# Cross-attention and a two-expert FFN on one core: the weights' loads and splits moved into the first batch

## The reference

```python
# attention: q = layernorm(x), k = v = ctx; 8 heads of 16 rows, softmax over 256 keys
qk = einsum('bhdq,bhdl->bhql', qh, kh) / sqrt(16)
x = x + gamma * einsum('bhql,bhdl->bhdq', softmax(qk), vh)
# FFN on xn = layernorm(x): two experts, each 256 -> 512 -> 256, chosen for each row by argmax
h0 = gelu(xn @ W0a.T + b0a);  out0 = h0 @ W0b.T + b0b
h1 = relu(xn @ W1a.T + b1a);  out1 = h1 @ W1b.T + b1b
x = x + where(argmax(xn @ Wg.T) == 0, out0, out1)
```

## Time and profile before

| what | value |
|---|---|
| time, median of 3 runs | 248.42 us (248.38 to 250.54) |
| time of the profiled execution | 248.95 us |
| its span | 247.1 us |
| PE busy | 219.7 us (89%) |
| DVE busy | 178.1 us (72%) |
| ACT busy | 144.6 us (59%) |
| POOL busy | 96.3 us (39%) |
| moved by DMA | 25.86 MB, 105 GB/s on average |

### The profile page before, as it was taken

The page is one execution under the profiler, slowest core; times in us unless marked ns, Lnnn a source line. Parts: engine busy times, 40 slices in busy tenths (PEclk is TensorE's granted clock), DMA queues, the critical chain, the costliest instruction groups (busy, mean ns, idle before and its releaser), DMA issues.

```text
span 247.1 us, 5173 instructions
## 1 busy us (share of the span) xinstructions
PE 219.7 (89%) x2001; PEld 171.3 (69%) x2001; DVE 178.1 (72%) x368; ACT 144.6 (59%) x217; POOL 96.3 (39%) x128
## 2 busy tenths in 40 slices
PE   0477988777898999999999999999999989979995
PEld 0344544444577888788878887888788877959995
DVE  7667476999875988698869886987597715445573
ACT  2012454856667758775877587758774786644140
POOL 8440231333984822482248224823361054032000
PEclk9999999886799999999999999999999999999999
DMA  4227777723330525161516250514111000000101
GB/s 170 100 71 246 247 298 224 273 90 129 88 131 36 183 66 175 10 233 64 176 25 216 65 175 21 178 49 150 20 49 53 16 24 3 21 21 3 41 5 42
DMA packets 18954, 25.86 MB, mean 105 GB/s; under 512 B 1946, under 2 KB 12530, under 8 KB 18674
## 3 DMA queue, kind: packets, MB, share of 16 engines
q1 hardware_dynamic: 17782, 22.63, 27.8%
q10 hardware_dynamic: 1148, 2.90, 3.3%
HBM read 11.28 MB, written 2.10 MB: 54 GB/s over the span
## 4 chain that ended last, share of the span: by engine, by line
PE 72%; DVE 12%; ACT 9%; issue 5%; POOL 0%; DVEq 0%; ACTq 0%; POOLq 0%
PE ff L822 18%; PE ff L852 11%; PE od L765 8%; PE st L753 8%; PE ff L863 6%; PE smax L741 5%; DVE nmax L396 4%; ACT P L600 4%; PE st L728 3%; PE od L773 3%; ACT hid L637 2%; PE od L780 2%; PE smax L714 2%; PE tr L795 1%; DVE qkst L184 1%
## 5 line engine op out<-in xcount | busy, mean ns | idle before, releaser
L600 ACT ACTIVATE P<-st 128x1024 f32<-128x1024 f32 x64 | 65.6, 1025 | 54.1 <-PE st L753 45.6
L396 DVE TENSOR_REDUCE nmax<-smax 128x4 f32<-128x1024 f32 x54 | 66.1, 1224 | 28.8 <-PE smax L741 28.2
L262 POOL TENSOR_TENSOR mv<-mv,power 128x1 f32<-128x1 f32 x31 | 18.3, 591 | 69.2 <-DVE mv L361 69.2
L280 POOL TENSOR_TENSOR hidL<-hid,hidH 128x1024 fp32r<-128x1024 f32 x13 | 31.0, 2387 | 20.6 <-DVE hidH L456 16.2
L822 PE MATMUL ff<-xnTh,w1h 128*128 128x256 f32 x128 | 37.5, 293 | 1.0 <-DVE y L494 1.0
L753 PE MATMUL st<-qkst 64*128 64x256 f32 x240 | 31.1, 338 | 6.6 <-ACT P L600 6.5
L637 ACT ACTIVATE hid<-ff,b1t 128x256 f32<-128x256 f32 x64 | 26.7, 470 | 17.4 <-PE ff L822 17.3
L822 PE MATMUL ff<-xnTh,w1l 128*128 128x256 f32 x128 | 36.0, 281 | 0.0
L822 PE MATMUL ff<-xnTl,w1h 128*128 128x256 f32 x128 | 35.9, 281 | 0.0
L765 PE MATMUL od<-P,vt 128*32 128x256 f32 x512 | 35.7, 426 | 0.1
L852 PE MATMUL ff<-w2h,hidH 128*128 128x256 f32 x124 | 34.2, 309 | 0.0
(11 more groups left out here) (100 smaller groups left out, 344.8 us busy)
## 6 DMA issues: line engine op xcount, KB each, us to landing
qkst<-parts SPq DMA_DIRECT2D x45, 256.0 KB
xv<-in_xv SPq DMA_DIRECT2D x16, 256.0 KB, 2.8
qk<-in_qk SPq DMA_DIRECT2D x15, 256.0 KB, 3.6
out<-y SPq DMA_DIRECT2D x16, 128.0 KB, 2.5
w1t<-in_w ACTq DMA_DIRECT2D x1, 1024.0 KB, 5.4
w2t<-in_w ACTq DMA_DIRECT2D x1, 1024.0 KB, 4.7
qk<-in_first SPq DMA_DIRECT2D x1, 256.0 KB, 3.8
qk<-in_first ACTq DMA_DIRECT2D x1, 256.0 KB, 3.9
```

The costliest lines, as they stand in the source:

```text
L262: pool.tensor_tensor(mv[:, b % 2, 11:12], mv[:, b % 2, 10:11], power[:, 0:1], ALU.pow).then_inc(s_rstd, 1)
L280: pool.tensor_tensor(hidL[:, units, :], hid[:, units, :], hidH[:, units, :], ALU.subtract).then_inc(s_hidL, 1)
L396: dve.tensor_reduce(nmax[:, c % 2, :, :, j].rearrange("p a e -> p e a"), (ff if c in WIDE and j % 2 else smax)[:, :, :, :], AX.X, ALU.max, ...
L600: act.activation(P[:, b % 2, j, :, :, :].rearrange("p e a l -> p (e a l)"), st[:, :, :, :].rearrange("p e a l -> p (e a l)"), ACT.Exp, sca ...
```

## The change

- `EARLY` gives batch 2 the slot -4 instead of -7. Its statistics, its q_norm, its high and low part and its stack copies come three slots later.
- ACT fills place 1 of `qkst` by two ACTIVATEs that read a broadcast constant; DVE fills place 2 alone, and makes the small memset of `onesb` in the head.
- ACT issues the load of w1 ahead of its loop, when the q and k of batch 2 have landed, and makes both halves of its high part there. The load of w2 is issued when the first stack (batch 1) has landed. ACT splits w2 in slots -1 and 0. The four small loads go from slot 0 to slot -2.
- POOL makes the low part of w1 ahead of its loop, before the `rstd` of batch 2, and that of w2 in slots 0 and 1.
- DVE's seven steps for gate and bias go from slots 6 to 12 to slots 0 to 6.

The diff, cut to its core:

```diff
-EARLY = {2: -7, 3: -2}
+EARLY = {2: -4, 3: -2}
@@ gpsimd, ahead of the loop, after the low part of batch 1's q
+            for half in range(LC):
+                pool.wait_ge(s_w1h, half + 1)
+                pool.tensor_tensor(w1l[:, half, :, :], w1t[:, half, :, :], w1h[:, half, :, :], ALU.subtract).then_inc(s_w1l, 1)
             rstd(2, mv1, 2, s_var1, s_rstd1)
@@ gpsimd, in the loop
                 if n == -1:
                     pad_values(0)
+                if 0 <= n < 2:
+                    pool.wait_ge(s_w2h, n + 1)
+                    half = slice(n * HM, (n + 1) * HM)
+                    pool.tensor_tensor(w2l[:, half, :], w2t[:, half, :], w2h[:, half, :], ALU.subtract).then_inc(s_w2l, 1)
...
-                if b == 3 and j >= 2:
-                    pool.wait_ge(s_w2h, j - 1)
-                    half = slice((j - 2) * HM, (j - 1) * HM)
-                    pool.tensor_tensor(w2l[:, half, :], w2t[:, half, :], w2h[:, half, :], ALU.subtract).then_inc(s_w2l, 1)
-                if b == 3 and j < LC:
-                    pool.wait_ge(s_w1h, j + 1)
-                    pool.tensor_tensor(w1l[:, j, :, :], w1t[:, j, :, :], w1h[:, j, :, :], ALU.subtract).then_inc(s_w1l, 1)
@@ vector
-            fill(dve, 1)
+            dve.memset(onesb[:, :], 1.0).then_inc(s_ones, 1)
             fill(dve, 2)
...
-                if 6 <= n < 13:
-                    gate_and_bias(n - 6)
+                if 0 <= n < 7:
+                    gate_and_bias(n)
@@ scalar, ahead of the loop
             act.dma_start(qk0[:, :, 1, :], first[1].rearrange("p (h l) -> p h l", h=2)).then_inc(s_c0, 16)
+            act.wait_ge(s_const, 1)
+            for side in range(2):
+
+                act.activation(qkst[:, 1, :, side, :], power[:, 0:1].unsqueeze(2).to_broadcast([128, PAIRS, L]), ACT.Copy,
+                               scale=-2.0 * side).then_inc(s_fill[1], 1)
             act.wait_ge(s_qk[0], 16)
...
             act.dma_start(qk0[DH:128:32, :, 1, :], ones0[:, :, :]).then_inc(s_one0, 16)
+
+            act.wait_ge(s_qk[1], 16)
+            act.dma_start(w1t[:, :, :, :].rearrange("p a e f -> p (a e f)"), w1).then_inc(s_w1, 16)
             act.wait_ge(s_qn, 1)
             act.activation(parts[:, 1, 1, :], qk[:, 0, 0, :], ACT.Copy).then_inc(s_hi, 1)
+            act.wait_ge(s_w1, 16)
+            for half in range(LC):
+                act.activation(w1h[:, half, :, :], w1t[:, half, :, :], ACT.Copy).then_inc(s_w1h, 1)
+            act.wait_ge(s_stk[0], stacked(1))
+            act.dma_start(w2t[:, :, :].rearrange("p u l -> p (u l)"), w2).then_inc(s_w2, 16)
@@ scalar, in the loop, after exp and copy_max0
-                if n == 0:
+                if -1 <= n < 1:
+                    act.wait_ge(s_w2, 16)
+                    half = slice((n + 1) * HM, (n + 2) * HM)
+                    act.activation(w2h[:, half, :], w2t[:, half, :], ACT.Copy).then_inc(s_w2h, 1)
+                for p in prepared(n - 2 if n > 0 else n - 1) if n else ():
+                    high(p)
+                if n == -2:
                     act.dma_start(wgb[:, :, :].rearrange("p a c -> p (a c)"), wg.partition_broadcast(128)).then_inc(s_small, 16)
...
```

More of the change, by code:

```diff
@@ L513, in gate_and_bias @@
                 if step == 5:
-                    dve.memset(onesb[:, :], 1.0).then_inc(s_ones, 1)
-                    dve.memset(bias_rows[:, :], 0.0).then_inc(s_ones, 1)
+                    dve.memset(bias_rows[:, :], 0.0).then_inc(s_bias, 1)
                 if step == 6:
-                    dve.wait_ge(s_bias, 4)
-                    dve.wait_ge(s_ones, 2)
+                    dve.wait_ge(s_bias, 5)
                     for n in range(3):
                         dve.tensor_copy(bias_rows[32 * n:32 * n + 1, :], bias_p[32 * n:32 * n + 1, n, :]).then_inc(s_bias, 1)
-            fill(dve, 1)
+            dve.memset(onesb[:, :], 1.0).then_inc(s_ones, 1)
             fill(dve, 2)
@@ L667, in _ @@
                     act.dma_start(b1t[:, :], b1).then_inc(s_small, 16)
[L668 to L680, removed]
                 if k == 0 and 2 <= c <= B:
@@ L830, in begin @@
                     pe.wait_ge(s_w2, 16)
-                    pe.wait_ge(s_bias, 7)
-                    pe.wait_ge(s_ones, 2)
+                    pe.wait_ge(s_bias, 8)
+                    pe.wait_ge(s_ones, 1)
                 pe.wait_ge(s_hid, UNITS * (b // 2) + (UNITS if t else UNITS - 2))
```

## The result

| | kernel before | changed kernel |
|---|---|---|
| median of 20 runs | 249.0 us (247.99 to 251.71) | 247.64 us (246.42 to 249.47) |
| ratio | 1 | 0.9937 (95% interval 0.9912 to 0.9963) |
| span of the profiled execution | 247.1 us | 246.3 us |

The change makes the kernel 0.6% faster, 1.6 us, where 0.4 us slower was forecast. The ratio lies near that of the means (249.3 and 247.8 us); the medians lie 1.4 us apart. The size is within 1%, as forecast most likely, but the interval excludes no change, and the sign is the other one.

A forecast was written before the change was run, and what follows sets the result against it. DVE was taken to bound the first third and PE the rest, so the first gemm's start decides. Terms -0.35 + 0.15 + 1.3 + 0.55 - 1.25 = +0.4 us gave a 248.8 us median, range 246.4 to 250.9.

The forecast's parts named there:

- part 1, the head: Fills, loads and statistics up to 17 us: ACT's fills let POOL's first pow start about 0.35 us earlier.
- the paragraph on the sum: Added the terms to +0.4 us at values(2); after it, x_norm's and q_norm's lost waits lie beside PE.
- Part 2: Early weight loads and splits: w1 lands near 11.9 us, POOL's split ends by 17.7; only w2's load costs, 0.15 us.
- Rival B: Slower: w1's load and the stack copies collide, w1 lands up to 3 us late, +2.25, 251.05 us; chance 0.10.
- Part 3: Port between DVE and POOL: POOL's w2 split blocks q_norm(4), perhaps the gate step; 0.65 to 1.1 us, 0.85 taken.
- Parts 3 and 4: Port blocking plus DVE's bias steps between the maxima: PE's transpose of batch 2 and values(0) come 1.3 us late.
- Part 5: DVE-bound stretch, n = 7 to 12: the steps that left it give back 1.25 us of chain.
- step 6: DVE's three copies, 0.90 us, between q_norm(5) and maximum (3,2), where wgd's 0.33 was: +0.55 us.
- The small transfer: Maxima row of batch 0 meeting w2's load: between nothing and 0.7 us, 0.15 taken.
- A: Faster by the clock and a free port: values(1) and values(2) gain, q_norm(4) not blocked, 246.6 us; chance 0.15.
- C: Whole gain: PE's idle time in DVE's stretch closes by all 2.7 us, early placement free, 245.4 us; chance 0.12.

The follow-up runs named there:

- b_head: Kernel before with EARLY[2] = -4 and ACT's fill of place 1, weights, gate and biases as before; ratio 0.9938 to the kernel before.
- a_pool_late: Changed kernel with POOL's four weight subtractions back at slots 12 to 15, loads and ACT's splits still early; ratio 0.9931 to the kernel before.
- b_gate: Kernel before with only the small loads moved to n = -2 and DVE's gate and bias steps to n = 0 to 6; ratio 1.0014.
- w_head: Changed kernel with POOL's w2 split at slots 4 and 5, bias steps in idle places, 72 small matmuls ahead of PE's loop; ratio 0.9903 to kernel before.
- a_gate_late: Changed kernel with the gate and bias steps back at n = 6 to 12, small loads still at n = -2; ratio 0.9930 to the kernel before.
- a_bias: Changed kernel with only DVE's steps moved: 0 to 2 at n = 0, 3 at n = 1, 4 to 6 at n = 5; ratio 0.9882, four runs.

## Why the prediction was wrong

**Step that failed first: part 1, the head.** It gave EARLY no term at all. Two edits were sized at 0.35 us together and measured 0.92: the fill 0.22 (the load landed 4.06 us after its issue, not 3.8) and EARLY 0.74. The rows were there: the maximum that ended at 13.31 and the matmuls that waited for it until 13.46. I had followed the chain, which names PE's matmuls of the third group (ended at 13.66) as what came last, and took the wait of the fourth for free. It was: but when the second maximum moved, part of the fourth group could run beside the third, and 0.74 us of chain went. With both edits b_head is by its ratio 1.5 us faster than the kernel before, not 0.35; of that 0.94 us are the head's own, and why the rest comes stays open.

**Step that failed second: the paragraph on the sum.** "x_norm and q_norm lose their waits for POOL, which lie beside PE" holds only while values(2) runs at the lower clock (8.89 against 8.84 us). At the upper one they are on the chain, 1.0 to 1.3 us (a_pool_late against the changed kernel). Even the chain before has the stopped q_norm on it, which the sentence denies:

```profile
65.59 0.65 DVE qk L385
```

I used the port's rows for the loss at q_norm(4) and not for the gain where they were read. That this gain reaches the time is not shown: a_pool_late has the changed kernel's ratio.

**What the two make of the error.** The forecast was +0.4 us: -0.35 for the head and +0.75 for all the rest. Measured were -1.5 us for the head alone (b_head) and nothing for the rest (b_head and the changed kernel have the same ratio), so 1.2 us of the error of 2.0 lie with the head and 0.75 with the rest, each known to about 0.8 us by the intervals.

**Right.** Part 2: w1 landed at 6.73 + 4.7 = 11.4 (11.9 forecast), POOL's split was over at 17.3 (17.7), ACT's fills ended at 4.73 (4.8), exp(0,0) followed the row as before. Rival B had no part in it. The first pow came at 6.20, not 6.0. Part 3: q_norm(4) 1.11 us, ending 0.15 behind the split, and wgd stopped as well, the upper bound. Parts 3 and 4 together: exp(0,0) to the transpose of batch 2 takes 16.11 instead of 14.70, +1.4, where 1.3 was forecast.

**Right in number only.** Part 5: from there to values(2) 0.9 came back; 0.7 (1.25 less the 0.55 of step 6) was forecast. But b_head, which moves no step, gains the same 0.9 there, so this can be luck of the clock. The small transfer: 0, its lower bound, in the changed kernel. In b_gate, with the four small loads beside it, scores0 waited 1.2 us longer, over my upper bound of 0.7. In w_head it waited 0.8, for a row that was issued 1.1 us earlier, while w2's load was farther from its end.

**Rivals.** A was half right: in the profiled execution values(2) ran at 1.93 us, but q_norm(4), which A had free, was stopped. And the gain doesn't hang on the clock alone, since b_head has it with values(2) at 3.64. C fell: up to values(2) 0.9 came back, not 2.7, and not surely by the steps' removal; b_gate and a_gate_late put the worth of moving them at nothing that can be measured.

**Open.** Whether the moves other than the head bring anything in the plain kernel. b_head and the changed kernel agree within 0.0001, with intervals of 0.003 on each side; a gain of 0.5 us could hide in that. Why the clock comes back up at the end of values(0) and not in the relay before it, with PE busy 3.6 of 4 us, isn't settled either.

## What to carry to other kernels

Look for every place where the moved operation stands now and where it will stand, and ask the same question of both: a port that costs 1 us at the new place can give it back at the old one, if the stopped operation is on the chain there. When an operation leaves an engine, shift everything behind it in the trace and look which wait on another engine starts to move, even if the chain names something else there. Where the clock's falls scatter the times by more than the effect, compare marks in the traces that lie ahead of the first fall, and use many executions for the rest.

## What the runs showed of the hardware that I had not expected

- The granted clock of a stretch reads 1.00 until the first event on record. Before 40 us scores0's matmuls took 2.08 us per slot at "1.00" in all kernels, and the same 2.08 in w_head, whose record says 0.50 there. So the first 36 us very likely run at 1.2 GHz in all kernels but w_head, and the column doesn't show it.
- 72 small matmuls in PE's idle first 7 us brought the clock up until 11.9 us (transpose at 14.90 instead of 15.98). Busy 18.6 of the 24 us after that, mostly with matmuls of 16 to 63 rows, PE stayed at the lower level.
- 8 small matmuls per slot in five slots, which do no useful work, went with two of the three lowest ratios of the case (0.9868 and 0.9883). The third, 0.9882, is a_bias, which has none.
- A DVE operation is stopped at each place to which POOL's work is moved: wgd (2.16 us for 0.41) and q_norm(4) (1.11 for 0.40) in slots 0 and 1, a bias subtraction (1.70 for 0.68) in slot 4.
